# Sixteen batches of conditioned attention on one core: attention output normalised in its transposed form, with row sums and rows carried by SBUF transfers

## What is computed

```python
def _sln(h, w, ...):                       # gamma, beta from the condition w of the batch
    ln = (h - mu) / jnp.sqrt(var + EPS) * ln_g + ln_b
    return gamma * ln + beta
h = _sln(hidden, w, ...)
qkv = (h @ Wqkv.T + bqkv).reshape(B, N, num_heads, hd, 3)
energy = jnp.einsum('bhqd,bhkd->bhqk', q, k)
att = jax.nn.softmax(energy, axis=-1) / D ** 0.5
out = jnp.einsum('bhqk,bhkd->bhqd', att, v)      # then (B, N, D)
h1 = out @ Wp.T + bp + hidden
h2 = _sln(h1, w, ...)
return h2 + h1
```

## Time and profile before

| what | value |
| --- | --- |
| median of 3 runs | 345.15 us |
| the profiled execution | 345.56 us |
| its span on the core | 343.8 us |
| PE busy | 332.5 us, 97% of the span |
| DVE busy | 298.3 us, 87% |
| ACT busy | 242.8 us, 71% |
| POOL busy | 159.1 us, 46% |
| granted clock of PE | 1.00 from the first slices to the last full one |
| DMA queue of SP | 46.74 MB, 49.2% of 16 DMA engines' span |

### The profile page before, as it was taken

How to read it: one execution, slowest core, us unless ns; L and a number is a source line. 1 busy time by engine, 2 the same in 40 slices (tenths; PEclk the granted TensorE clock), 3 DMA queues, 4 the chain that set the end, 5 groups by cost and what they waited for, 6 DMA issues and landing times.

```text
span 343.8 us, 8981 instructions
## 1 busy us (share of the span) xinstructions
PE 332.5 (97%) x3173; PEld 286.8 (83%) x3173; DVE 298.3 (87%) x728; ACT 242.8 (71%) x476; POOL 159.1 (46%) x187
## 2 busy tenths in 40 slices
PE   8888999999999999999999999999999999999993
PEld 4677879888888988888888988888898988888773
DVE  4888978799898989899898989989898988999684
ACT  7664876868676786868686876868687786766740
POOL 5765544437164545527264644617254643224330
PEclk9999999999999999999999999999999999999999
DMA  7396445456555454555545454655556354652021
GB/s 242 126 218 186 124 115 140 129 155 157 170 141 156 134 152 135 173 156 170 142 125 169 134 155 134 184 142 160 161 135 157 98 157 123 182 146 67 16 61 61
DMA packets 47705, 48.87 MB, mean 142 GB/s; under 512 B 6287, under 2 KB 41374, under 8 KB 47662
## 3 DMA queue, kind: packets, MB, share of 16 engines
q1 hardware_dynamic: 44494, 46.74, 49.2%
q10 hardware_dynamic: 1184, 1.07, 1.2%
q0 software_dynamic: 1984, 0.51, 0.8%
HBM read 9.99 MB, written 4.23 MB: 41 GB/s over the span
## 4 chain that ended last, share of the span: by engine, by line
PE 87%; DVE 5%; DMA 3%; ACT 1%; issue 1%; ACTq 1%; SPq 0%; DVEq 0%
PE m L976 24%; PE st L976 19%; PE sa L976 18%; PE pv L976 17%; PE pv L1065 4%; DVE mx L692 3%; PE pv L1146 2%; PE m L1105 2%; DMA wqkv<-WqkvT_dram 2%; DMA kst<-qk_l 1%; PE pv L1079 1%; PE m L1079 1%; ACT p L602 0%; DVE qk_l L727 0%; ACTq L625 0%
## 5 line engine op out<-in xcount | busy, mean ns | idle before, releaser
L692 DVE TENSOR_REDUCE mx<-sa 128x2 f32<-128x512 f32 x256 | 171.5, 684 | 28.4 <-PE sa L976 27.3
L602 ACT ACTIVATE p<-st 128x512 f32<-128x512 f32 x240 | 140.9, 598 | 37.5 <-PE st L976 33.2
L976 PE MATMUL sa<-kst,qst 126*128 126x256 f32 x512 | 105.6, 288 | 2.0 <-DMA kst<-qk_l 1.0
L976 PE MATMUL st<-qst,kst 128*128 128x256 f32 x496 | 104.1, 292 | 0.2
L976 PEld LDWEIGHTS st<-qst,kst 128*128 128x128 f32 x496 | 75.1, 188 | 13.8 <-issue 12.8
L976 PEld LDWEIGHTS sa<-kst,qst 126*128 126x128 f32 x512 | 78.6, 189 | 4.6 <-DVE mx L692 1.7
L368 POOL DMA_DIRECT2D qst<-m_h x31 | 17.6, 567 | 112.4 <-DVE m_l L701 112.4
L976 PE MATMUL pv<-p,v_st 128*32 128x256 f32 x1008 | 61.0, 382 | 0.0
L976 PEld LDWEIGHTS pv<-p,v_st 128*32 128x32 f32 x1008 | 29.5, 109 | 21.0 <-ACT p L602 1.5
L976 PE MATMUL m<-hT_h,wqkv_h 128*128 128x256 f32 x128 | 36.8, 300 | 1.3 <-ACT hT_h L616 0.7
L377 POOL TENSOR_SCALAR xn<-xa,mv,rstd 128x256 f32<-128x256 f32 x28 | 34.2, 1227 | 1.5
(11 more groups left out here) (149 smaller groups left out, 566.2 us busy)
## 6 DMA issues: line engine op xcount, KB each, us to landing
qst<-qk_h SPq DMA_DIRECT2D x64, 128.0 KB, 2.4
qst<-qk_l SPq DMA_DIRECT2D x64, 128.0 KB, 2.5
kst<-qk_h SPq DMA_DIRECT2D x62, 128.0 KB, 2.5
kst<-qk_l SPq DMA_DIRECT2D x62, 128.0 KB, 2.8
xa<-x_dram SPq DMA_DIRECT2D x16, 256.0 KB, 3.0
gb<-gb_rows SPq DMA_DIRECT2D x16, 256.0 KB, 3.9
out_dram<-y SPq DMA_DIRECT2D x15, 256.0 KB, 3.4
wqkv<-WqkvT_dram SPq DMA_DIRECT2D x1, 512.0 KB, 5.6
```

What stands on the lines that cost most here:

```text
L602: nc.scalar.activation(p32[:, h, :], st_ps[h % 2][:], ACT.Exp).then_inc(exp_done, 1)
L692: dve.tensor_reduce(mx[:, par(a), h // HH, (h % HH) * TT:(h % HH + 1) * TT], sa_ps[h % 2][:].rearrange("p (t n) -> p t n", t=TT), AX.X, AL ...
L976: return nc.tensor.matmul(o, l, r, start=start, stop=stop)
```

## The change

For batches 0 to 13 (`by_transfer`), the attention output stays transposed:

- `out_by_token`, `normalise` by tokens and `turn_att` are left out. v is laid out so that channels and sums alternate on the partitions, and the channels of v and the rows of the projection's weight are reordered to suit (`by_rows`).
- SP sends the sums of each half as 64 pieces of 32 numbers to a small tile `sums` (128x32), and the channels of each half to `o_rows` (64 partitions; 128x512 for both) (`send_out`). DVE takes the reciprocal of `sums` ahead of maximum 6 (`reciprocal`). SP gathers it into 16 rows (`gather_rec`, two transfers) and spreads these over 128 partitions (`spread_rec`, 256 KB). That makes seven transfers more per step.
- DVE multiplies the 128x512 in SBUF by the spread reciprocals, ahead of maximum 14 (`normalise`). ACT makes `aT_h` from the SBUF tile in slot 15, POOL makes `aT_l` (`low_att` on POOL, slot 15).
- The projection of the batch moves from slots 12 to 15 of step `b` to slot 15 of step `b` and slots 0, 1 and 1 of step `b + 1`, and its products are put in the order high by high, high by low part of the weight, low part last.
- q's products are ordered in the same way, and the first two quarters of them move from slots 0 and 1 to slots 12 and 13 of the step before. The statistics of x (`norm1`) move from slots 4 and 5 to 11, 12 and 13 of the step before, and `low_max` and the last stage of the residual one place ahead, to behind maximum 10.
- Batches 14 and 15 go the old way (`normalise_tokens`). In `finish`, both halves of the last output are turned after both have been normalised; before, the first was turned early.

```diff
-Q_SLOTS, K_SLOTS, V_SLOTS, P_SLOTS = (0, 1, 3, 4), (4, 5, 5, 6), (7, 7, 8, 8), (12, 13, 14, 15)
-S_MT1, S_AT, S_MT0, S_XT = 1, 10, 9, 10
+Q_SLOTS, K_SLOTS, V_SLOTS, P_SLOTS = (12, 13, 3, 4), (4, 5, 5, 6), (7, 7, 8, 8), (15, 0, 1, 1)
+S_MT1, S_AH, S_MT0, S_XT = 1, 15, 9, 10
...
+            def send_out(a, g):
...
+                sp.wait_ge(oT_ready, 2 * a + g + 1)
+                wait(sp, recs_in, 32 * a)
+                sp.dma_start(sums[half_rows, :], oT[1:P:32, g, :]).then_inc(sums_in[g], 16)
+                wait(sp, aTh_ready, a - 1)
+                wait(sp, aTl_ready, a - 1)
+                sp.dma_start(o_rows[par(a)][half_rows], oT[0:P:2, g, :].rearrange("p (c n) -> p c n", c=2)).then_inc(o_in[g], 16)
...
+                sp.wait_ge(rec_ready, a + 1)
+                for n in range(2):
+                    sp.dma_start(recs[n:2 * HH:2, :], sums[:]).then_inc(recs_in, 16)
...
+                sp.wait_ge(recs_in, 32 * (a + 1))
+                wait(sp, rows_ready, a)
+                sp.dma_start(o_rec[:], recs.rearrange("r (d n) -> r d n", d=1)
+                             .broadcast_to([2 * HH, HD // 2, 2 * N])).then_inc(rec_in, 16)
...
+                dve.tensor_tensor(o_rows[par(a)], o_rows[par(a)], o_rec[:], ALU.mult).then_inc(rows_ready, 1)
...
-                    if h == S_AT + 1 and has(b - 1):
-                        wait(act, attT_done, 1 * (b - 1) + 1)
+                    if h == S_AH and has(b - 1):
+                        wait(act, rows_ready, 1 * (b - 1) + 1)
...
+            def low_att(a):
+
+                wait(pool, aTh_ready, a + 1)
+                pool.tensor_tensor(aT_l[:], o_rows[par(a)], aT_h[:], ALU.subtract).then_inc(aTl_ready, 1)
...
-                    (7, 0): [lambda: normalise(b - 1, 1, 0)],
+                    (6, 0): [lambda: reciprocal(b - 1)],
...
+                    (12, 1): [lambda: norm1(b + 4, 1)],
+                    (13, 1): [lambda: norm1(b + 4, 2)],
+                    (10, 1): [lambda: low_max(b + 1, 0), lambda: residual(b - 2, 5)],
+                    (11, 0): [lambda: norm1(b + 4, 0)],
+                    (14, 0): [lambda: normalise(b - 1)],
```

213 lines of the change are left out of this document (137 added, 76 removed).

## The result

The kernel after takes 362.37 us (median of 4 runs, 360.68 to 364.93), against 346.3 us for the kernel before, measured beside it (345.02 to 347.54, 4 runs). The ratio is 1.0485, with a 95% interval of 1.0445 to 1.0525: slower by about 5%. The prediction was 343.2 us, with a range of 337 to 350 us. It was wrong.

The account below looks back on a forecast made before the run. PE, busy 97%, was taken as the bound. Step and end terms, -0.45 - 1.2 - 1.65 - 0.5 + 0.2 + 0.65 + 0.65 = -2.3 us, took the profiled 345.56 to 343.3 us, set at 343.2 us for the median; range 337 to 350 us.

Parts of the forecast that it names:

- PE's own work falls to 18.15 us: Per step on PE: three groups of transposes, 1.35 us, go from a 19.50 us step, leaving 18.15 us of work.
- The chain in slots 13 to 15: From slot 13's `sa` through maximum 13, `normalise` and `aT_h`: 2.74 us against 1.55 us of PE work, so PE waits 1.2 us.
- A step of 19.35 us: Whole step: 18.15 us of PE work plus 1.20 us of wait in slot 15, 0.15 us less than before.
- SP's queue, slack of 1.0 us: SP's last send lands at 18.6 us, and slot 0 of the next step reads it at 19.6 us: 1.0 us slack.
- rival 2: SP's queue becomes the bound: held sends land 0.8 to 1.7 us late for slot 0; 353 up to 365 us; chance 0.13.
- Covered by the wait in slot 15: PE's slot 15 wait covers SP's last send; without that wait PE would stall in slot 0 by about 0.2 us.
- The spread is there by 16 us: In each step the spread is issued at about 11.9 us and lands by 16 us; `normalise` starts at 17.4 us.
- Its rival with waits of PE: Late sends make PE wait in slot 0: 13 x 0.8 = 10 us more, 353 us, up to 365 us; chance 0.13.
- The reciprocal and the sums in time: Sums issued at about 5.3 us need 1.9 us; the reciprocal stands at about 8.75 us, so they are 1.5 us early.
- rival 3: POOL's 1.28 us product blocks `normalise` on DVE, both reading SBUF: 14 x 1.28 = 18 us more, 361 us; chance 0.02.
- The ends: `last_step` +0.65 us, as triples return to it, and `finish` +0.65 us (0 to 1), as its first low half comes later.
- The removed transposes: 168 transposes removed from PE, worth 18.5 us, of which nearly everything goes into 14 waits.

## Why the prediction was wrong, point by point

- **PE's own work falls to 18.15 us: right.** With q's last quarters in slot 14 the short steps take 18.55 us, with 0.22 us of wait and 0.15 us of load behind it: 18.2 us. In the kernel after it is 18.3 us.
- **The chain in slots 13 to 15: right.** 1.2 us of wait was forecast with the load in it, 1.05 to 1.45; measured with 0.15 us of load it is 1.08 us without the spread and 1.26 us in the kernel after, where 2.6 us in all come from the spread's being late for `normalise`. Each link took what its row said: 0.66, 0.68 and 0.63 us. The 0.11 us for the load was 0.15 us.
- **A step of 19.35 us: right without the spread** (19.3 us), and wrong with it (19.8 to 22.5 us, 20.6 us on average).
- **SP's queue, slack of 1.0 us: the step that failed.** The sum gave each issue 0.65 us and took the holds of the earlier trace rows for rare. It counted the spread's bytes like any others. But while the spread reads partitions 0 to 15, the pair of sends behind it is held by 1.3 us or more in each step (2.60 us for a pair in the step shown), which is more than the slack. The hold was set at 0 and cost 9.0 us of waits for k and 2.0 us of loads, 2.6 us more in slot 15, and the half clock, 5.1 us in the profiled execution. This is the place, the condition (over 1.0 us held per step) and the price (353 up to 365 us) of rival 2, which had a chance of 0.13. Rival 2 did not have the reason: it spoke of holds that more transfers bring, and six more transfers without the spread cost nothing (345.9 us). Nothing in the trace of before shows 256 KB read from 16 rows of SBUF, so the hold should have been bounded from both sides, and no bound was given.
- **"Covered by the wait in slot 15": half right.** The wait covers a part of SP's last sends and the maxima's rows; without it both come out (374.3 us with slots 0, 0, 1, 1). It didn't cover the held 1.4 us.
- **The spread is there by 16 us: nearly.** DVE waited for it five times, 2.4 us in all.
- **The clock wasn't in the forecast.** Its rival with waits of PE did not carry the half clock, about 5 us in the profiled execution. What brings it is not shown (see the last section).
- **The reciprocal and the sums in time: right without the spread**, where in most steps the sums are issued 5.3 to 6.0 us and the reciprocal starts 8.75 us behind the first scores of slot 0, as forecast. In the kernel after the sums go out at 6.5 us and later, and three waits of DVE (1.5 us in all) are the result; the gather then stands ahead of the sends. POOL under `normalise` (rival 3): did not come, 0.68 us.
- **The ends: +1.3 us forecast with `last_step` and `finish`, 2.45 us measured** from the copy of step 14 on. In that stretch also lie the wait in slot 15 of step 14 (1.34 us) less a group of transposes (0.47 us), which the forecast has in step 14. `finish` itself: from the last `weigh` of eight heads to the last `y`, 344.19 to 358.37 us here and 325.51 to 338.99 us before, +0.7 us against +0.65.
- **The removed transposes.** The prediction puts them at 18.5 us; by its own 1.35 us per step they are 14 x 1.35 = 18.9 us. Nothing hangs on it, since its sum goes by steps.
- **The value of the whole: less than forecast even when repaired.** Without the spread the kernel takes what the kernel before takes (ratio 0.9999) and not 2 us less: its steps are 0.2 us shorter, and its start and its ends take back the 2.9 us. With the spread spaced it takes 348.9 us. The transposes go into 14 waits, as the forecast said, until something fills them.

## What to carry to other kernels

When work moves from an engine to transfers, ask of each new transfer which partitions it reads, not only how many bytes it has; here 16 rows that are read eight times each were cheaper 4 or 7 partitions apart. A product taken from the engine that bounds the kernel is worth something only on the stretch that is bound: here the stretch from slot 7 to slot 0 is set by sends, and the stretch from slot 13 to 15 by a chain, so the gain came by moving other products into the wait there. An operation that waits for a transfer is to stand as late as its reader lets it, since all of its engine stands behind it: DVE's reciprocal waited 22.5 us in the run that had it one maximum earlier.

## What the runs showed of the hardware

- A transfer of 256 KB inside SBUF lands in 5.2 us from partitions 0 to 15 that are each read eight times, in 3.5 us from 16 partitions that are 4 or 7 apart, and in 2.8 us as a copy from 128. The issue of the next pair of sends takes 2.48 to 3.40 us in the first case. With rows 7 apart and with the copy it takes 1.2 us in about half of the steps and 1.45 to 2.5 us in the others. With the first kind of spread in ACT's queue a pair of SP's takes 2.2 to 4.2 us in ten steps.
- Pairs are held now and then without any spread, too: 15 of 97 took 1.8 to 2.3 us in the kernel without it, in place of 1.2 us.
- PE's granted clock fell to half (1.2 GHz) three times in the kernel after, for about 3.5 us each, and came back by itself while PE was busy. Ahead of the first two falls PE had idled 1.58 and 0.79 us, and 1.07 and 0.79 us; ahead of the third 1.31 us. But 1.43 and 0.83 us, and 1.32 and 0.82 us, left it at 1.00, so the length of the waits alone does not tell when it falls. One wait of 0.9 us per step alone left the clock at 0.999 (without the spread).
- The issue of a transfer takes 0.55 to 0.62 us of ACT's own time, about what it takes in SP's queue (0.59 us for the spread).
